# One-pass products of parts in the routed down projection, and what is moved to make room for them

## The reference, cut to what matters

```python
x = x + tanh(g_xattn[0]) * cross_attention_0(ctx, layernorm(x))
x = x + tanh(g_ffn[0]) * ffn_0(layernorm(x))
# ffn_0, for each of the 896 rows, 8 experts, the two best of them used:
scores = sigmoid(xf @ gate_w + bias); w = the two best scores, normalised
hact = gelu(xf @ up_w[e] + up_b[e], exact)          # 256 -> 1024
combined = sum_e w[e] * 0.1 * (hact @ down_w[e] + down_b[e])   # 1024 -> 256
shared = 0.1 * (gelu(xf @ sw_up + sb_up) @ sw_down + sb_down)
out = (shared + combined) / (max|shared + combined| + 1e-6)
```

## Time and profile before

| | us |
|---|---|
| median of 3 runs (761.78 to 762.6) | 762.36 |
| the profiled execution | 762.74 |
| its span | 760.9 |
| TensorE busy | 730.7 |
| VectorE busy | 462.4 |
| ScalarE busy | 387.1 |
| GpSimd busy | 187.3 |

### The profile page before, as it was taken

One profiled execution on the slowest core, in us unless ns is written; L12 is line 12 of the kernel. 1 busy time (PEld: TensorE's weight loads), 2 busy tenths in 40 slices (PEclk: granted clock), 3 DMA queues, 4 the chain that ended last, 5 costly groups with the idle time before them and its releaser, 6 DMA issues.

```text
span 760.9 us, 15119 instructions
## 1 busy us (share of the span) xinstructions
PE 730.7 (96%) x5426; PEld 592.3 (78%) x5426; DVE 462.4 (61%) x1152; ACT 387.1 (51%) x1014; POOL 187.3 (25%) x317
## 2 busy tenths in 40 slices
PE   9999999999998998999999999989999999999998
PEld 8567777777775787999999996666777667889988
DVE  3788788887776331132232225947878887798754
ACT  3676766766756421332323322677887889121131
POOL 4131321312000062000000005654455527411000
PEclk9999999999999999999999999999999999999999
DMA  4332323432120893367655514340000000000001
GB/s 166 102 81 65 88 83 109 116 89 77 35 50 5 279 334 120 119 206 248 221 195 195 173 58 126 94 164 2 3 2 2 2 2 3 1 1 1 0 7 43
DMA packets 43533, 69.77 MB, mean 92 GB/s; under 512 B 6611, under 2 KB 35036, under 8 KB 43204
## 3 DMA queue, kind: packets, MB, share of 16 engines
q1 hardware_dynamic: 41924, 65.14, 27.2%
q0 software_dynamic: 1536, 3.67, 1.6%
HBM read 52.56 MB, written 8.26 MB: 80 GB/s over the span
## 4 chain that ended last, share of the span: by engine, by line
PE 81%; DVE 9%; ACT 4%; issue 3%; DMA 1%; SPq 1%; POOL 0%; ACTq 0%; DVEq 0%; POOLq 0%
PE ps L1473 11%; PE ps L1738 10%; PE ps L1752 10%; PE ps L1954 7%; PE ps L1535 5%; PE ps L1538 5%; PE ps L1662 4%; PE ps L1836 3%; PE ps L1577 3%; PE ps L1651 3%; PE ps L1780 3%; PE ps L1790 3%; PE ps L1597 3%; PE ps L1989 2%; PE ps L1478 2%
## 5 line engine op out<-in xcount | busy, mean ns | idle before, releaser
L780 ACT ACTIVATE OT<-ps,bt 128x128 f32<-128x128 f32 x168 | 47.9, 368 | 103.1 <-PE ps L1738 102.2
L1473 PE MATMUL ps<-ident,arena 112*122 112x112 f32 (+5 forms) x584 | 81.6, 274 | 5.5 <-ACT rt L822 3.8
L1473 PEld LDWEIGHTS ps<-ident,arena 112*122 112x122 f32 (+5 forms) x584 | 63.6, 154 | 28.9 <-issue 14.5
L992 DVE TENSOR_REDUCE negmax<-ps 112x1 f32<-112x375 f32 x128 | 61.2, 540 | 31.0 <-PE ps L1836 31.0
L1738 PE MATMUL ps<-OT,arena 128*128 128x128 f32 x672 | 78.5, 275 | 0.0
L1954 PE MATMUL ps<-arena_r 128*112 128x384 f32 x384 | 75.7, 345 | 1.9 <-DVE acc L1262 1.0
L1738 PEld LDWEIGHTS ps<-OT,arena 128*128 128x128 f32 x672 | 76.8, 192 | 0.1
L1752 PE MATMUL ps<-arena,OT 128*128 128x256 f32 x336 | 75.8, 379 | 0.0
L1186 DVE COPY yo<-ps 128x256 f32<-128x256 f32 x21 | 8.9, 425 | 103.8 <-PE ps L1752 103.8
L1752 PEld LDWEIGHTS ps<-arena,OT 128*128 128x128 f32 x336 | 62.3, 190 | 7.6
L1954 PEld LDWEIGHTS ps<-arena_r 128*112 128x112 f32 x384 | 63.7, 175 | 4.0 <-DVE arena L1395 1.2
(11 more groups left out here) (291 smaller groups left out, 1480.8 us busy)
## 6 DMA issues: line engine op xcount, KB each, us to landing
arena<-in_up_w SPq DMA_DIRECT2D x21, 1024.0 KB, 5.2
arena<-in_down_w SPq DMA_DIRECT2D x8, 1024.0 KB
arena<-arena SPq DMA_DIRECT2D x128, 60.9 KB, 2.0
arena<-in_wqkv SPq DMA_DIRECT2D x1, 3072.0 KB, 10.5
arena<-in_ctx SPq DMA_DIRECT2D x8, 375.0 KB
slot_rows<-acc SPq DMA_DIRECT2D x6, 448.0 KB, 3.5
OT<-slot_rows SPq DMA_DIRECT2D x21, 128.0 KB, 2.1
slot_out<-yo SPq DMA_DIRECT2D x21, 128.0 KB, 1.7
```

Of the source, the lines that this page charges most:

```text
L780: act.activation(he[:, i % 2, m, :], ps[:, 2 * (i % 2) + m // 4, (m % 4) * SLOT:(m % 4 + 1) * SLOT], ACT.Gelu, bias=bt[:, i % 3, m:m + 1]) ...
L992: dve.tensor_reduce(negmax[0:TQ, h % 4:h % 4 + 1], ps[0:TQ, S_BANKS[h % 4], 0:TK], AX, ALU.max, negate=True)\
L1473: return pe.transpose(dst, src, ident[0:k, 0:k])
```

## The change

1. `e_down` multiplies by parts: for each of the 8 blocks three one-pass products (`he_hi` x `hi`, `he_hi` x `lo`, `he_lo` x `hi`), so 24 matmuls of 256 columns instead of 16 passes. It waits for the low parts of half a tile (`s_helo`) instead of each gelu.
2. ScalarE computes each gelu twice, into the float32r `he_hi` and the float32 `he`, and copies the first 3 of 8 blocks of a tile's down weights into their high part, after a register load.
3. VectorE copies the other 5 blocks (two copies in odd tiles), then subtracts all 8 for the low part (two subtractions in even tiles, four in odd ones), and subtracts twice 512 columns for `he_lo`.
4. The parts need room: the up weights keep two buffers, so the load of tile i + 2 waits for the up of tile i. It now stands behind the loads of `near` and `w1` in SyncE's program, and `far` behind the last store.
5. VectorE no longer prepares the weights of tiles 0 and 1 ahead of the loop: `e_rows(0)` and `e_rows(1)` stand first, `e_down_w(0)` follows, and `e_down_w(1)` comes in the loop behind the low parts of tile 0.
6. At the joint `sw_low(0)` goes from step u = 2 to the end of u = 3, and `sw_low(1)` behind `l0_norm(6)`. `sh_up` takes its four products with the high weights first; `sh_up(0)` waits for the second `sw_low` ahead of the sixth product alone.

```diff
-        (wd, wu_0, wu_1, wu_2, wdc_0, wdc_1) = layout(
-            0, [P, E0, FM * D], [P, KC, FF], [P, KC, FF], [P, KC, FF], [P, FM, D], [P, FM, D])
+        (wd, wu_0, wu_1) = layout(0, [P, E0, FM * D], [P, KC, FF], [P, KC, FF])
+        (he_hi, wd_hi_0, wd_lo_0, wd_hi_1) = layout(20480, [P, 2, FM, SLOT], [P, FM * D], [P, FM * D], [P, 5 * D], of=arena_r)
+        wd_hi = (((0, 3, wd_hi_0[:, 0:3 * D]), (3, 8, wd_hi_0[:, 3 * D:])),
+                 ((0, 3, wd_hi_1[:, 0:3 * D]), (3, 5, wd_hi_1[:, 3 * D:]), (5, 8, xnT_r[:, 0:3 * D])))
+        wd_lo = (((0, 3, wd_lo_0[:, 0:3 * D]), (3, 8, wd_lo_0[:, 3 * D:])), ((0, 3, wT_r[:, 0:3 * D]), (3, 4, cos_t_r[:, 0:D]), (4, 5, sin_t_r[:, 0:D]),
+                                      (5, 8, xnT_r[:, 3 * D:6 * D])))
...
             def e_up_load(i):
-                if i >= 3:
-                    sp.wait_ge(s_eup, 2 * (i - 3) + 2)
+                if i >= 2:
+                    sp.wait_ge(s_eup, 2 * (i - 2) + 2)
...
-            sp.wait_ge(s_eup, 2 * NTILE)
-            sp.dma_start(far, a["ctxT"][NEAR:, :, :].rearrange("b (c p) k -> p b c k", p=P)).then_inc(s_far, 16)
             sp.wait_ge(s_ye, NTILE)
             sp.dma_start(ys[(NTILE - 1) * SLOT:, :], yo[:, (NTILE - 1) % 2, :]).then_inc(s_yst[(NTILE - 1) % 2], 16)
+            sp.dma_start(far, a["ctxT"][NEAR:, :, :].rearrange("b (c p) k -> p b c k", p=P)).then_inc(s_far, 16)
...
+            def e_down_w(i):
+                if i >= 2:
+                    act.wait_ge(s_edown, i - 1)
...
+                e = act.value_load(owni[0:1, i:i + 1], min_val=0, max_val=E0 - 1)
+                act.activation(wd_hi[i % 2][0][2], wd[:, bass.ds(e, 1), 0:3 * D].rearrange("p a n -> p (a n)"), ACT.Copy)\
+                   .then_inc(s_kvhi, 1)
...
-                    act.activation(he[:, i % 2, m, :], ps[:, 2 * (i % 2) + m // 4, (m % 4) * SLOT:(m % 4 + 1) * SLOT],
-                                   ACT.Gelu, bias=bt[:, i % 3, m:m + 1]).then_inc(s_egelu, 1)
+                    act.activation(he_hi[:, i % 2, m, :], src, ACT.Gelu, bias=bt[:, i % 3, m:m + 1])
+                    act.activation(he[:, i % 2, m, :], src, ACT.Gelu, bias=bt[:, i % 3, m:m + 1]).then_inc(s_egelu, 1)
+                if 0 < i < NTILE - 1:
+                    e_down_w(i + 1)
...
+                for lo, hi, v in wd_hi[i % 2][1:]:
+                    link(dve.tensor_copy(v, of_expert(lo, hi)))
+                dve.wait_ge(s_kvhi, E_HIGH + i + 1)
+                for lo, hi, v in wd_lo[i % 2]:
+                    ins = dve.tensor_tensor(v, of_expert(lo, hi),
+                                            rows_of(wd_hi[i % 2], lo, hi).bitcast(F32), ALU.subtract)
+                ins.then_inc(s_wdc, 1)
...
             for i in range(NTILE):
                 if i and i + 1 < NTILE:
                     e_rows(i + 1)
+                he_low(i, 0)
                 if i:
                     e_take(i - 1)
-                    if i + 1 < NTILE:
-                        e_down_w(i + 1)
+                he_low(i, 1)
+                if i + 1 < NTILE:
+                    e_down_w(i + 1)
...
                 for m in range(FM):
-                    pe.wait_ge(s_egelu, i * FM + m + 1)
-                    ins = pe.matmul(ps[:, 4 + i % 2, 0:D], he[:, i % 2, m, :], wdc[i % 2][:, m, :], start=(m == 0),
-                                    stop=(m == FM - 1))
+                    if m % 4 == 0:
+                        pe.wait_ge(s_helo, 2 * i + m // 4 + 1)
+                    hi, lo = rows_of(wd_hi[i % 2], m, m + 1), rows_of(wd_lo[i % 2], m, m + 1)
+                    for k, (xv, wv) in enumerate(((he_hi, hi), (he_hi, lo), (he_lo, hi))):
+                        ins = pe.matmul(ps[:, 4 + i % 2, 0:D], xv[:, i % 2, m, :], wv, start=(m == 0 and k == 0),
+                                        stop=(m == FM - 1 and k == 2))
```

More of the change, by code:

```diff
@@ L61, in build @@
         ident = sb("ident", [P, P])
+        with nc.sbuf_tensor("cos_t_r", [P, NK0], F32R) as cos_t_r:
+            pass
         cos_t = sb("cos_t", [P, NK0])
+        with nc.sbuf_tensor("sin_t_r", [P, NK0], F32R) as sin_t_r:
+            pass
         sin_t = sb("sin_t", [P, NK0])
@@ L97, in build @@
         wtok = sb("wtok", [TQ, B, E0 + 1])
+        with nc.sbuf_tensor("wT_r", [P, TOK], F32R) as wT_r:
+            pass
         wT = sb("wT", [P, TOK])
@@ L200, in build, with rows_of @@
         xsq = wbuf0[:, 2048:2048 + KC * TOK].rearrange("p (c q) -> p c q", c=KC)
-        (wd, wu_0, wu_1, wu_2, wdc_0, wdc_1) = layout(
-            0, [P, E0, FM * D], [P, KC, FF], [P, KC, FF], [P, KC, FF], [P, FM, D], [P, FM, D])
-        wu, wdc = (wu_0, wu_1, wu_2), (wdc_0, wdc_1)
+        (wd, wu_0, wu_1) = layout(0, [P, E0, FM * D], [P, KC, FF], [P, KC, FF])
+        wu = (wu_0, wu_1)
+        (he_hi, wd_hi_0, wd_lo_0, wd_hi_1) = layout(20480, [P, 2, FM, SLOT], [P, FM * D], [P, FM * D], [P, 5 * D], of=arena_r)
[3 more added lines that the diff above has]
+                                      (5, 8, xnT_r[:, 3 * D:6 * D])))
+        he_lo = OT_r[:, 0:2048].rearrange("p (k m n) -> p k m n", k=2, m=FM)
+        def rows_of(parts, lo, hi):
+            for a, b, v in parts:
+                if a <= lo and hi <= b:
+                    return v[:, (lo - a) * D:(hi - a) * D]
         sw_u = wbuf0[:, 0:FM * D].rearrange("p (c n) -> p c n", c=KC)
@@ L252, in build @@
         s_shw, s_wd = sem("shared_w_loaded"), sem("down_w_loaded")
-        s_wu = [sem(f"up_w_loaded_{k}") for k in range(3)]
+        s_wu = [sem("up_w_loaded_even"), sem("up_w_loaded_odd")]
         s_up, s_gelu, s_down, s_acc = (sem(n) for n in ("sh_up", "sh_gelu", "sh_down", "sh_acc"))
@@ L1078, in l0_step @@
                     x_low(n - 2)
-                if n == B - 1 and u == 2:
-                    sw_low(0)
                 if n == B - 1 and u == 3:
                     l0_rows(n - 1)
-                    sw_low(1)
+                    sw_low(0)
             l0_rope(0, 0)
@@ L1089, in _ @@
             l0_norm(6)
+            sw_low(1)
             l0_logits(6)
@@ L1644, in sh_up @@
                 half, m = u // FM, u % FM
-                pe.wait_ge(s_shlo, B + 2 if half else B)
+                pe.wait_ge(s_shlo, B + 2 if half else B - (u == 0))
                 if u >= 2:
@@ L1648, in sh_up @@
                 q = slice(half * 4 * TQ, (half + 1) * 4 * TQ)
-                for c in range(KC):
-                    for k, (wv, xv) in enumerate(((sw_u_hi, xnT_hi), (sw_u_hi, xnT_lo), (sw_u_lo, xnT_hi))):
-                        ins = pe.matmul(ps[:, u % 2, 0:4 * TQ], wv[:, c, m * P:(m + 1) * P], xv[:, c, q],
-                                        start=(c == 0 and k == 0), stop=(c == KC - 1 and k == 2))
+                products = ((0, sw_u_hi, xnT_hi), (0, sw_u_hi, xnT_lo), (1, sw_u_hi, xnT_hi), (1, sw_u_hi, xnT_lo),
+                            (0, sw_u_lo, xnT_hi), (1, sw_u_lo, xnT_hi))
+                for k, (c, wv, xv) in enumerate(products):
+                    if u == 0 and k == 5:
+                        pe.wait_ge(s_shlo, B)
+                    ins = pe.matmul(ps[:, u % 2, 0:4 * TQ], wv[:, c, m * P:(m + 1) * P], xv[:, c, q],
+                                    start=(k == 0), stop=(k == 5))
                 ins.then_inc(s_up, 1)
```

33 lines of the change are left out of this document (23 added, 10 removed).

## The result

The changed kernel took 756.9 us (median of 5 runs, 755.42 to 758.18) beside 762.6 us of the kernel before on the same chip (5 runs, 761.78 to 765.68): a ratio of 0.9914, 95% interval 0.9889 to 0.9939. Faster, as forecast, but 5.7 us instead of 13, and above the range of 745.5 to 755.

The account below looks back on a forecast made before the run. TensorE, busy 96% of the span, was taken to bound the kernel. Terms -12.8 + 1.1 - 1.0 - 0.4 = -13.1 us from 762.74 gave 749.6, stated as 749.5, with an 8-in-10 range of 745.5 to 755.

Parts of the forecast that it names:

- The down products: Experts' loop: 24 one-pass products take 2.85 us instead of 16 passes in 3.46, saving 12.8 us over 21 tiles.
- The other engines: Experts' loop: VectorE's 5.7 to 6.0 us and ScalarE's 5.5 to 5.8 per tile fit within TensorE's 6.64.
- The choice on the copy: VectorE's high-part copy of 1280 columns keeps 0.6 ns a column with a float32r target, 0.77 us rather than 1.47.
- The first tiles: Start of experts' loop: TensorE waits 1.1 us (0.5 to 2) ahead of tile 2's up for VectorE's rows.
- The joint: Ahead of the shared expert: TensorE's 0.92 us wait goes, transposes of l0_x(6) come 1.0 us sooner (0.8 to 1.1).
- the rival: At the joint the granted clock holds, 1.9 us more come back, 747.6 us in all; chance 0.18.
- it falls again, since the longest gap stays: At the joint 1.7 us of idle time remains, so the granted clock was taken to fall again, with nothing regained.
- Behind the experts: After the last down: last store goes ahead of far, gathers start sooner; 0.4 us gained (0.8 gain to 1 loss).
- the sum: Whole kernel: -12.8 + 1.1 - 1.0 - 0.4 = -13.1 us, from 762.74 to 749.6.
- a saving that other waits eat up: Rival without a given place: the saved time is lost to other waits; chance 0.02.

Follow-up runs that it names:

- bursts kernel of group 4: Changed kernel with GpSimd's scatters in bursts of 6, 5 and 5, first two tiles' row transposes behind block 14's down product: 745.48 us, ratio 0.9822.
- group 0: First measurement, on one chip: changed kernel as it is against the kernel before, 756.9 us beside 762.6, ratio 0.9914.
- the kernel before with bursts: Kernel before with its scatters in bursts of 6, 5 and 5, against the unaltered kernel before: 758.58 us beside 758.89, ratio 0.9998.
- the changed kernel of group 5: Changed kernel as it is, run a third time, against the kernel before on the same chip: 744.96 us beside 758.15, ratio 0.9829.
- the groups 4 and 5: Runs without late signals: changed kernel as it is, with bursts, eight scatters or a copy among scatters, 743.73 to 745.48 us; kernel before 758.89 and 758.15.
- The joint and the missing copy: Two variants of the kernel before: sooner joint alone, 764.68 us, 1.0024; VectorE's copy of tile 0's down weights moved from among the scatters, 770.23 us, 1.0027.
- the direct copies: Changed kernel with GpSimd's 16 indirect scatters replaced by 16 direct copies of the same bytes from SyncE, rows in wrong slots: 746.5 us, ratio 0.9783.
- fewer signals: Shared down products signal once per half, second w_T pair moved behind the scatters: changed kernel 753.36 us, ratio 0.9891; kernel before 763.96 us, ratio 1.0016.
- the groups 0 to 3: Runs showing late signals, each group on one chip: changed kernel as it is took 756.9 and 757.24 us; kernel before 762.6, 761.56, 768.01 and 761.54.

## Why the prediction was off, step by step

**The down products: right.** 2.85 us was forecast for 24, 2.83 to 2.84 came. The loop is 11.97 us shorter, where -12.8 + 1.1 = -11.7 was said. It is 139.8 us in every variant of the changed kernel, on every chip.

**The other engines: right.** VectorE has 4.96 to 5.45 us of work in a tile (5.7 to 6.0 forecast), ScalarE 5.1 (5.5 to 5.8). Both forecasts had the idle time for a register in them, which a busy time has not. The choice on the copy was the right one, it keeps its rate with a float32r target:

```profile
349.33 0.82 DVE L1216 CAST arena_r<-arena 128x1280 fp32r x1
```

**The first tiles: right.** Chain of work, first transposes for tile 2 and its up:

```profile
320.82 0.38 PE ps L1521 x2
321.20 0.59 issue
321.79 3.81 PE ps L1789 x32
```

0.59 of waiting, and 0.24 and 0.16 more in the pieces beside it than 3.57 and 0.22: 1.0 us, forecast 1.1.

**The joint: the wait right, the clock not foreseeable.** The transposes of `l0_x(6)` start at 240.46 instead of 241.68, 1.2 us sooner (over all profiles 240.22, mean of 15, against 241.38, mean of 5: 1.16). The row, to be held against the earlier trace rows:

```profile
240.46 0.41 PE L1521 MATMUL ps<-ident,xn 112*128 112x112 f32 x2 [1.72 <-DVE xn L1048]
```

The idle time of 1.71 to 1.74 us is there in all 20 profiles. Behind it the granted clock fell in 7 of them and held at 1.00 in 13: with the old joint it fell in 3 of 5, with the new in 4 of 15. From those transposes to `sh_up(9)` it is 34.4 us where it held, 36.0 where it fell (so holding is worth 1.6 us, where the rival had 1.9), 37.5 in the bursts kernel of group 4, where it stayed at 0.50 from 242 to 248:

```profile
246.00:248.00 2.00, 2.00 (x6) 1.69 (x6) 0.00 (x0) 1.96 (x4) 0.00 (x0) 0.50 0.00 0
```

The step "it falls again, since the longest gap stays" took one execution for a rule. The same gap was followed by the fall in some executions and not in others. In the two profiled executions of group 0 this gave 1.6 us to the changed kernel, which a median need not see.

**Behind the experts: right where signals are on time.** Between the kernel before with bursts and the changed kernel of group 5 the span behind the last down is 303.0 against 302.6 us, so 0.4 less, as said, and the last store lands in 1.9 instead of 3.0 us. In group 0 it was 1.1 us more: GpSimd gathers there, ScalarE waited 3.74 us for a product of line 1834, and the store took 3.7 us.

**The step that failed** is one that the sum made in silence: the stretch from `sh_up(9)` to the first expert was taken over whole, at nothing, since the change touches little in it. It measured +7.7. It lies between two edits that do touch it: one moves the work ahead of it by 1.2 us, the other takes VectorE's copy from among the scatters. The kernel before had there two waits of ScalarE for TensorE that its own products don't explain (the lines of 3.74 and 4.65 us above). They were not asked about. Its three runs on record then lay within 0.8 us and gave no sign; two later ones took 765.4 and 765.7. So no rival had this form, a stall that is small before and large after; the nearest, "a saving that other waits eat up", had 0.02 and no place. What the runs showed in place of nothing is that TensorE's signals come up to 10.9 us late while GpSimd scatters. On the chips of the groups 4 and 5, where they don't, the sum holds: 758.15 - 13.1 = 745.05, and 744.96 was measured. That it fits within 0.1 us is partly luck. The clock held in all five executions of the changed kernel there, against the forecast, and in seven of ten of the kernel before; with the median of those seven, 757.54, the difference is 12.6.

**What stays open:** why some chips hold TensorE's signals back and others don't; what sets the length, from 3.1 to 11.8 us; why it is 10.9 us in the changed kernel and 3.1 in the kernel before; whether it takes GpSimd's issuing, its queue's packets or the recording. The joint and the missing copy seem to add to it, by ratios of 1.0024 and 1.0027 that only just clear 1 and by profiles on different chips; neither is shown, nor by what path it would act.

## To carry to other kernels

A wait whose releaser had long ended by its own row ("remote", or a releaser that finished microseconds before) can be a late signal; the recorded time of the semaphore's update tells. A stretch that has one is not a constant of the sum: price what the change does to it, or say that it can grow (here from 3.1 to 10.9 us). Keep chains of short steps between TensorE and ScalarE away from a row of indirect DMAs where you can, as the direct copies did; fewer signals helped the changed kernel here, and not the kernel before. Compare a change of 1% with the kernel before on more than one chip: the same two programs differed by 5.7 us on one and by 13.2 on another.

## What the runs showed of the hardware

- While GpSimd issues indirect DMAs one after the other (0.94 us each, 1.25 apart), TensorE's semaphore updates reached ScalarE up to 10.9 us late in the groups 0 to 3, and never late in the groups 4 and 5. It begins after some seven issues and ends within 2.9 us of the last one. ScalarE's recorded signals were on time meanwhile (in the kernel before 283.93 for a gelu that ended at 283.92, and 289.63 for 289.62), though one or two of each kernel left no record. Direct copies of the same bytes from SyncE did nothing of the kind (746.5 us, where the changed kernel without its joint took 757.83 in the same group).
- It does not hang on how much the DMA engines carry: at 92 to 95 GB/s in the stretches above, the gelu waited 13.53 us, and 13.48 with the weights' loads running for the first third of it.
- After the same idle time of 1.72 us the granted clock fell to its lower level in 7 of 20 executions.
